# Which engine issues the copies of a layer norm's result: ScalarE in place of SyncE

## The reference

```
h   = relu(layernorm(x))                          # 50000 x 256
agg = segment_sum(edge_attr, dst, 50000) / max(count, 1)   # 50000 x 64
out = x + relu(concat([agg, h]) @ W1 + b1) @ W2 + b2       # W1 320x512, W2 512x256
```

## Time and profile before

| | |
|---|---|
| time, median of 3 runs | 1353.75 us (1352.83 to 1354.43) |
| the profiled execution | 1355.23 us, span of its instructions 1353.3 us |
| TensorE busy | 1326.5 us (98%), mean granted clock 0.992 |
| VectorE busy | 1209.9 us (89%) |
| ScalarE busy | 695.7 us (51%) |
| GpSimd busy | 541.3 us (40%) |
| moves HQ<-HN | 388 issues by SPq, 128 KB each, 3.2 us from issue to landing |

### The profile page before, as it was taken

One profiled execution on the slowest core, in us unless ns is written; L12 is line 12 of the kernel. 1 busy time (PEld: TensorE's weight loads), 2 busy tenths in 40 slices (PEclk: granted clock), 3 DMA queues, 4 the chain that ended last, 5 costly groups with the idle time before them and its releaser, 6 DMA issues.

```text
span 1353.3 us, 29713 instructions
## 1 busy us (share of the span) xinstructions
PE 1326.5 (98%) x6968; PEld 1119.2 (83%) x6968; DVE 1209.9 (89%) x3059; ACT 695.7 (51%) x1281; POOL 541.3 (40%) x710
## 2 busy tenths in 40 slices
PE   4999999999999999999999999999999999999999
PEld 2778888888888888888888888888888888888887
DVE  5889899989999998999899999999999999989997
ACT  3545555555555554545454545454545455555553
POOL 6433434344343434343434343434343434343431
PEclk7999999999999999999999999999999999999999
DMA  4454555555554545454545454545454545455542
GB/s 111 102 139 117 136 119 134 121 132 125 127 130 123 133 120 133 120 132 120 134 118 138 114 145 109 145 110 145 111 142 113 141 115 138 117 136 119 134 109 76
DMA packets 422724, 168.59 MB, mean 125 GB/s; under 512 B 321188, under 2 KB 422326, under 8 KB 422712
## 3 DMA queue, kind: packets, MB, share of 16 engines
q1 hardware_dynamic: 421720, 167.28, 50.6%
q10 hardware_dynamic: 992, 1.18, 0.3%
HBM read 66.12 MB, written 51.40 MB: 87 GB/s over the span
## 4 chain that ended last, share of the span: by engine, by line
PE 94%; SPq 2%; POOL 1%; DMA 1%; issue 1%; DVE 1%; ACT 0%; POOLq 0%; DVEq 0%
PE P L914 27%; PE P L916 13%; PE P L891 13%; PE P L893 13%; PE P L892 13%; PE P L900 6%; PE P L901 6%; PE PA L880 1%; PE PA L879 1%; SPq L307 0%; SPq L309 0%; DMA dst_w<-in_dst_dram 0%; PE PA L875 0%; SPq L308 0%; SPq L275 0%
## 5 line engine op out<-in xcount | busy, mean ns | idle before, releaser
L914 PE MATMUL P<-w_both,H_hi 128*128 128x512 f32 x1564 | 558.5, 398 | 2.3 <-DVE H_lo L719 2.3
L598 ACT ACTIVATE H_hi<-P 128x512 fp32r<-128x512 f32 x392 | 233.5, 596 | 505.6 <-PE P L901 505.6
L916 PE MATMUL P<-w_both,H_lo 128*128 128x256 f32 x1564 | 440.4, 282 | 0.0
L914 PEld LDWEIGHTS P<-w_both,H_hi 128*128 128x128 f32 x1564 | 294.7, 188 | 74.7 <-DVE H_lo L719 2.8
L719 DVE SCALAR_TENSOR_TENSOR H_lo<-P,H_hi 128x512 fp32r<-128x512 f32 x392 | 266.4, 680 | 83.7 <-ACT H_hi L598 80.7
L891 PE MATMUL P<-HT_hi,w_hi 128*128 128x512 f32 (+1 forms) x784 | 312.4, 398 | 1.9 <-ACT w_both L612 1.9
L893 PE MATMUL P<-HT_hi,w_lo 128*128 128x512 f32 (+1 forms) x784 | 308.0, 393 | 0.0
L892 PE MATMUL P<-HT_lo,w_hi 128*128 128x512 f32 (+1 forms) x784 | 306.0, 390 | 0.0
L438 POOL TENSOR_TENSOR XB<-X,b_row 128x1024 f32<-128x1024 f32 x98 | 237.6, 2425 | 169.6 <-DVE O L733 165.9
L916 PEld LDWEIGHTS P<-w_both,H_lo 128*128 128x128 f32 x1564 | 294.4, 188 | 3.8
L432 POOL TENSOR_TENSOR E_both<-ES,E_both 128x256 fp32r<-128x256 f32 x98 | 73.0, 745 | 403.5 <-ACT E_both L578 403.5
(11 more groups left out here) (77 smaller groups left out, 1157.1 us busy)
## 6 DMA issues: line engine op xcount, KB each, us to landing
HQ<-HN SPq DMA_DIRECT2D x388, 128.0 KB, 3.2
out_dram<-O SPq DMA_DIRECT2D x97, 512.0 KB, 3.3
X<-in_x_dram SPq DMA_DIRECT2D x96, 512.0 KB, 3.5
ER<-in_edge_attr_dram SPq DMA_DIRECT2D x392, 32.0 KB, 1.7
DT<-table_dram SPq DMA_DIRECT2D x392, 1.0 KB, 1.7
X<-in_x_dram ACTq DMA_DIRECT2D x1, 512.0 KB, 4.7
w_raw<-in_L_gnn_W_dram ACTq DMA_DIRECT2D x4, 128.0 KB, 4.9
w_raw<-in_L_gnn_W_dram SPq DMA_DIRECT2D x2, 256.0 KB, 3.9
```

The costliest lines, as they stand in the source:

```text
L598: act.activation(H1_hi[:, m, nodes(t)], bank(m)[:, nodes(t)], ACT.Relu).then_inc(s_1hi, 1)
L914: pe.matmul(out_bank(j)[some, :], H1_hi[:, m, rows], w2_both[:, m, :, :].rearrange("p a d -> p (a d)"), start=(m == 0), stop=False)
L916: last = pe.matmul(out_bank(j)[some, 0:D], H1_lo[:, m, rows], w2_both[:, m, 0, :], start=False, stop=(m == CH - 1))
```

## The change

The function `move` and its calls leave SyncE's sequence and come into ScalarE's. There each call stands behind the `layernorm` of its tile: directly behind it for tiles 1, 2 and 3, and behind `edges_high` of that tile in the loop. The wait on `s_ln` stays, as does everything that reads `s_hq`.

```diff
@@ block.sync
-            def move(t, b):
-                sp.wait_ge(s_ln, SUB * t + SUB)
-                into_quadrants(sp, b)
...
             load_windows(1, 1)
-            move(1, 1)
             load_x(3, 1)
             load_windows(2, 0)
-            move(2, 0)
             load_windows(3, 1)
             store(0, 0)
             load_x(4, 0)
             load_windows(4, 0)
-            move(3, 1)
             store(1, 1)
             with sp.Fori(1, TILES // 2 - 2) as i:
...
-                    move(2 * i + (h + 2), h)
                     store(2 * i + h, h)
...
-                if t + 2 < TILES:
-                    move(t + 2, t % 2)
@@ block.scalar
+            def move(t, b):
+                act.wait_ge(s_ln, SUB * t + SUB)
+                into_quadrants(act, b)
...
             layernorm(1, 1)
+            move(1, 1)
             edges_high(0, 0)
...
             layernorm(2, 0)
+            move(2, 0)
             transposed_high(1)
...
             layernorm(3, 1)
+            move(3, 1)
             edges_high(3, 1)
             with act.Fori(1, TILES // 2 - 1) as i:
...
                     layernorm(2 * i + (h + 2), h)
                     edges_high(2 * i + (h + 2), h)
+                    move(2 * i + (h + 2), h)
```

## The result

| | median us | runs | lowest to highest |
|---|---|---|---|
| before | 1353.41 | 7 | 1352.41 to 1355.60 |
| changed | 1358.85 | 7 | 1358.26 to 1359.59 |

The ratio is 1.0043 with an interval of 1.0034 to 1.0053: 5.4 us slower, and just outside my range, which ended at 1358.5.

What follows compares the result with a forecast made beforehand. TensorE, full in the loop, was taken as the bound, with the loop costing 0. The start summed 0.86 + 1.48 + 1.0 - 2.31 - 1.61 = -0.58 us, giving 1353.2 us against 1353.75; 8-in-10 range 1350.0 to 1358.5.

Steps and rivals of the forecast that it cites:

- What bounds the kernel: Loop from 100 to 1300 us: TensorE is full at full clock, so any gain lies before 80 us.
- the hole before tile 1: Start, TensorE's first matmul of tile 1: waits for HT_lo behind tile 2's moves until 47.32, a new hole of 1.48 us.
- that at the edge matmuls: Start, tile 3: E_both behind the moves delays GpSimd's subtraction, a second new TensorE hole of 1.0 us.
- the first delay: Start: tile 1's moves stand before E_both of tile 0, making TensorE's first edge matmul 0.86 us later.
- No hole near 72 us: Start, H_lo of tile 2's last slice: tile 3's HQ lands earlier, so TensorE's old hole of 2.31 us goes.
- So the lateness is swallowed there: Loop: H_lo is 0.75 us late, VectorE's 0.79 us pause per tile at the third slice absorbs it, cost 0.
- slack of 0.45 at QA: Loop, TensorE's first matmul with QA: another 0.45 us of cover, so H_lo may be 1.24 us late.
- Rival (b): ScalarE in the loop: past 3.35 us from layer norm's end to H_hi, TensorE has a hole every tile, 1363; chance 0.13.
- The price: Loop: cover passed by 0.1 us a tile costs 94 x 0.1 = 9.4 us.
- The term of 1.61 us for the clock: Start, after the hole near 72 us: a stretch at 1.2 GHz costing 1.61 us disappears with the hole.
- Rival (a): ScalarE's issues before the loop: cheap at 0.45 us each, -2.9 us, 1350.9; chance 0.17.
- Rival (c): Loop, HQ landing: moves run beside the store and land later; an excess of 0.1 gives 9.4 us, 1363; chance 0.05.

Runs made afterwards that it cites:

- the run with QA first: Changed kernel with VectorE's two instructions that make QA ahead of the residual of group 0, in the loop and last tiles: 1358.76 us, ratio 1.0043.
- the ten idle instructions: Kernel before, SyncE issuing all moves, with ten extra ScalarE copy instructions per tile of the loop behind E_both: 1380.33 us, ratio 1.0204.
- the run with two places: Kernel before with ScalarE issuing tile 3's moves and the loop's, there two behind E_both and two behind the next tile's first H_hi: 1350.37 us, ratio 0.9982.
- The run with the start alone: Kernel before with only the moves of tiles 1 to 3 issued by ScalarE, SyncE keeping all in the loop: 1354.99 us, ratio 1.0018.
- the run with five issues: Changed kernel with five issues per tile instead of four, the first quadrant in two halves of 16 partitions, same bytes: 1421.70 us, ratio 1.0507.

## Why the prediction was wrong

**What bounds the kernel, and the sizes of the start's holes: right in kind.** An issue takes 0.66 us, E_both of tile 0 started at 32.09 (said 32.2), the hole before tile 1 ends at 47.85 (said 47.3) and is 1.82 us (1.48), that at the edge matmuls 1.24 (1.0), the first delay 0.99 - 0.20 = 0.79 (0.86). The moves of tile 2 took 3.24 us and not 2.73, which makes the difference at tile 1. No hole near 72 us, as said.

**"So the lateness is swallowed there": the step that failed.** I let the layer norm end at a fixed moment, put 2.7 us of issues behind it, found the H_lo 0.75 us late, and set against that VectorE's pause of 0.79 and a slack of 0.45 at QA, as if each tile began anew. It doesn't: VectorE, when it has no pause left behind the first H_lo, brings HT later, ScalarE its layer norm later, and the next H_hi is later by that too. Before, the first H_lo starts 0.18 us ahead of the tile's first edge matmul in one half of the loop and 0.33 in the other; in the changed kernel 0.97 and 0.82 behind it. That is 1.15 us late in both, and not 0.75, and 0.17 and 0.27 of it is the layer norm itself, which now ends 2.80 and 2.70 us ahead of that matmul and not 2.97.

The bound isn't a slack at one reader but the length of the circle, 10.48 us and the gap. Before, its spare of 1.63 us stood in two places: the first H_hi waited 0.75 us longer to be taken up than the 0.63 it needs, and VectorE took 6.95 us from the first H_lo to the end of the transpositions where 6.06 are work. Those two I had, nearly (0.79 for the second). The 0.45 at QA isn't on the circle, and I added it all the same; the run with QA first shows that it was worth nothing. So the gap may be 13.447 - 10.48 = 2.97 us where I had named 3.35, and the real gap was 3.01. Rival (b) is what happened, in the place I gave it, 0.04 us past a point that I had put 0.4 too far. The price was right: 0.04 us a tile is 3.8 us. The part of the gap that I had taken too small (2.9 in my sum) is what the sequencer does between its last issue and H_hi: 0.42 us in one half of the loop (714.63 to 715.05) and 0.17 in the other.

**The term of 1.61 us for the clock: mis-sized.** It stood in one profile, and I took it as part of every execution; that execution took 1355.23 us, 1.5 over the median against which I set the gain. In the second, of 1353.23 us, it is nought. Without it my own sum is +1.03, and the measured one +2.0: the two new holes are 0.34 and 0.24 us longer than said, and the one removed is 2.1 and not 2.31. The run with the start alone says 1.0018.

**Rival (a)**, cheap issues, is refuted by 0.66 us. **Rival (c)**, landings: the median went from 3.1 to 3.2 us, the longest from 3.8 to 4.7, and VectorE waited for HQ once in the loop, 0.4 us; the ten idle instructions made the same kind of loss with no DMA moved, and the run with two places had none with every issue of the loop in ScalarE's queue.

Together: 3.8 us in the loop and about 2 in the start make 5.8, and 5.4 were measured.

## What to carry to other kernels

When one engine is full and others wait for it, look for circles among the others before putting work on one: add up the work from an instruction round to its next turn, without the waits, and compare it with the period. The spare of the circle is one number, the sum of the pauses along it (here 0.75 + 0.88); slack at a reader that isn't on the circle, as TensorE's at QA, adds nothing to it. A circle that is longer than the period by a little falls back by that much in every tile, until the bound engine waits for it. Where a trace calls the bound engine 100% busy, count its instructions in a fixed stretch or take the time from start to start; here 21 matmuls of 6339 told what busy time and waits didn't. And what only one profile shows of the clock isn't a term of a sum.

## What the runs showed of the hardware

- Six copies of 128x256 by ScalarE from one constant tile took 1.94 us, 0.32 each, while the layer norm's four of the same size, with a scale and a bias per partition, took 2.06, 0.51 each.
- The issue of a move of 128 KB over 32 partitions takes ScalarE's sequencer 0.66 us and SyncE's 0.64; in the run with five issues the two over 16 partitions took 0.60 and 0.64 us and those over 32 took 0.65 to 0.67, so half the partitions wasn't half the time.
- ScalarE's sequencer issues DMAs while the engine computes (the second pair at 707.29, beside the H_hi from 707.28), but what stands behind the issues waits for them: H_hi began 0.17 or 0.42 us after the last of four.
- A hole of 2.31 us in TensorE was followed by a stretch at 1.2 GHz that cost 1.6 us in one execution of the kernel before, and one of 2.1 us by none in another. In the run with the start alone a hole of 2.33 us was followed by such a stretch too, in the changed kernel one of 1.82 us by none.
